# Attention in a fused layer: six heads of eight scored as three products of halves, and three copies per batch moved to another engine

## The reference

```python
q = rope(rmsnorm(x @ Wq))            # 32 query heads of 128
k, v = rope(rmsnorm(x @ Wk)), x @ Wv # 8 key heads of 128
k_all = concat(k_cache[block_table], k)   # 16 pages of 32 keys, 32 new ones: 544
v_all = concat(v_cache[block_table], v)
scores = (q . k_all) / sqrt(128), masked beyond the cache length
o = softmax(scores) @ v_all          # 4 query heads share a key head
x + o @ Wo
```

## Time and profile before

| what | value |
|---|---|
| median of 3 runs | 2431.99 us (2431.39 to 2432.4) |
| the profiled execution itself | 2430.95 us |
| its span | 2429.2 us |
| busy in the span: TensorE, VectorE, ScalarE, GpSimd | 95%, 74%, 55%, 47% |
| attention, by the timeline | 829 to 2057 us |

### The profile page before, as it was taken

One profiled execution on the slowest core, in us unless ns is written; L12 is line 12 of the kernel. 1 busy time (PEld: TensorE's weight loads), 2 busy tenths in 40 slices (PEclk: granted clock), 3 DMA queues, 4 the chain that ended last, 5 costly groups with the idle time before them and its releaser, 6 DMA issues. The chain is left out here.

```text
span 2429.2 us, 50595 instructions
## 1 busy us (share of the span) xinstructions
PE 2318.3 (95%) x14977; PEld 1934.9 (80%) x14977; DVE 1790.6 (74%) x3412; ACT 1344.7 (55%) x2635; POOL 1145.5 (47%) x1330
## 2 busy tenths in 40 slices
PE   6997899999999499999999999999999998899999
PEld 5335777777777399999999999999999997788887
DVE  4565189999999588888888888888888886522221
ACT  6563388888887355555555555555555554421111
POOL 0320044444444376777776777777777675000000
PEclk9998999999999699999999999999999999999999
DMA  9335323333332688888888888888888885843441
GB/s 313 99 102 177 103 66 108 109 109 108 108 104 79 196 280 298 289 280 290 297 289 290 277 291 288 297 294 281 285 292 296 286 292 172 256 133 96 129 138 60
DMA packets 463993, 501.42 MB, mean 206 GB/s; under 512 B 102069, under 2 KB 396981, under 8 KB 457654
## 3 DMA queue, kind: packets, MB, share of 16 engines
q1 hardware_dynamic: 427062, 366.37, 47.6%
q0 software_dynamic: 36864, 134.23, 15.8%
HBM read 404.02 MB, written 96.47 MB: 206 GB/s over the span
## 5 line engine op out<-in xcount | busy, mean ns | idle before, releaser
L1092 POOL TENSOR_TENSOR att_probs<-att_probs,att_inverse 128x512 f32<-128x512 f32 x512 | 535.1, 1045 | 289.1 <-DVE att_inverse L1288 284.5
L1196 ACT ACTIVATE att_probs<-att_probs,att_low 128x544 f32<-128x544 f32 x512 | 383.9, 750 | 515.8 <-DVE att_low L1275 454.7
L1153 PE MATMUL att_o<-att_probs_t,att_values 128*128 128x128 f32 x4096 | 540.9, 275 | 0.0
L1275 DVE CUSTOM_DVE_ANT_0 att_probs<-att_score,att_mask,att_batch_cols 128x544 f32<-128x544 f32 x512 | 399.9, 781 | 138.3 <-PE att_score L1118 99.6
L1153 PEld LDWEIGHTS att_o<-att_probs_t,att_values 128*128 128x128 f32 x4096 | 497.6, 192 | 0.0
L1284 DVE COPY att_probs_t<-att_turn 128x512 f32<-128x512 f32 x512 | 350.8, 685 | 1.2 <-PE att_turn L1133 1.2
L1078 POOL DMA_INDIRECT att_values<-L_cond_v_cache,att_v_rows_of x256 | 283.7, 1108 | 82.4 <-POOL att_v_rows_of L1074 49.7
L1118 PE MATMUL att_score<-att_keys_raw,att_queries_raw 128*128 128x288 f32 (+1 forms) x1024 | 290.7, 407 | 29.0 <-DMA att_queries_raw<-q_t 26.8
L1133 PE MATMUL att_turn<-ident,att_probs 128*128 128x128 f32 x2048 | 311.1, 274 | 1.2 <-POOL att_probs L1092 0.9
L787 PE MATMUL proj_proj<-x3t_hi,proj_w_hi 128*128 128x512 f32 x640 | 266.7, 417 | 6.9 <-DVE proj_w_lo L847 6.9
L1251 DVE TENSOR_TENSOR att_keys_lo<-att_keys_raw,att_keys_hi 128x384 fp32r<-128x384 f32 (+1 forms) x320 | 259.8, 812 | 17.6 <-ACT att_keys_hi L1189 17.6
(11 more groups left out here) (132 smaller groups left out, 4008.6 us busy)
## 6 DMA issues: line engine op xcount, KB each, us to landing
att_keys_raw<-L_cond_k_cache SPq DMA_DIRECT2D x1024, 128.0 KB
q_t<-proj_q_out SPq DMA_DIRECT2D x32, 1024.0 KB, 3.9
att_queries_raw<-q_t SPq DMA_DIRECT2D x64, 512.0 KB
o_t<-att_heads_out SPq DMA_DIRECT2D x64, 512.0 KB
out_o_raw<-o_t SPq DMA_DIRECT2D x32, 1024.0 KB, 5.8
prep_natural<-L_cond_weight SPq DMA_DIRECT2D x16, 1024.0 KB, 8.4
w_nat<-L_cond_Wq SPq DMA_DIRECT2D x8, 1024.0 KB, 5.4
v_new<-values_v_out SPq DMA_DIRECT2D x64, 128.0 KB, 2.0
```

The lines of the kernel that those rows point to most:

```text
L1092: nc.gpsimd.tensor_tensor(probs[:, k, 0:L], probs[:, k, 0:L], inverse[:, k:k + 1].to_broadcast([P, L]), ALU.mult).then_inc(probs_ready, 1)
L1153: last = nc.tensor.matmul(o, values[j][:, t, h * D:(h + 1) * D], probs_t[m % 2][:, t * P:(t + 1) * P], start=(t == 0), stop=False, skip_gr ...
L1196: nc.scalar.activation(probs[:, k, :], probs[:, k, :], ACT.Exp, bias=low[k][:, 0:1], scale=-1.0, accum_out=total[k][:, 0:1]).then_inc(exp_ ...
L1275: nc.vector.tensor_tensor_reduce(out=probs[:, k, :], in0=score_ps[:, LEFT:LEFT + KEYS], in1=mask[j][:], scale=batch_cols[j][:, h:h + 1], s ...
```

## The change

Two heads of eight stay native in place of four, so `SPLIT` is six, and each part of the keys is 3 pages of six heads (576 columns; the last part 2 pages, 384 columns), in six parts in place of five; the queries are 768 columns in place of 512. ScalarE begins with the next batch in head 1 in place of 4, VectorE in head 2 in place of 5. The copy of the turned weights goes to ScalarE for heads 1, 4 and 7 of a batch; ScalarE makes it two heads later, ahead of the exponent of that later head. VectorE keeps the other five. Since `NATIVE` is 2, the next load of keys is issued after three scored heads in place of five, and TensorE waits for the halves at head 2.

```diff
-    NATIVE = 4
-    ACT_FROM, DVE_FROM = 4, 5
+    NATIVE = 2
+    ACT_FROM, DVE_FROM = 1, 2
+    KEPT_BY_ACT = (1, 4, 7)
     SPLIT = HK - NATIVE
-    PARTS = [slice(0, 3), slice(3, 6), slice(6, 9), slice(9, 13), slice(13, NPP + 1)]
+    PARTS = [slice(0, 3), slice(3, 6), slice(6, 9), slice(9, 12), slice(12, 15), slice(15, NPP + 1)]
...
# ScalarE
+            def main_part(i, n):
+                m = n % N
+                back = i if n >= 0 else i - 1
+                act.wait_ge(turned, i * N + (n + 1))
+                act.wait_ge(weighed[m % 2], back * (N // 2) + m // 2)
+                nc.scalar.activation(probs_t[m % 2][:], turn_ps[:], ACT.Copy).then_inc(kept, 1)
...
             def pair(i, first, last_pair):
                 for n in range(N):
                     j, h = divmod(n, HK)
+                    if (n - 2) % HK in KEPT_BY_ACT and (n >= 2 or not first):
+                        main_part(i, n - 2)
                     softmax(i, n)
...
             pair(PAIRS - 1, False, True)
+            main_part(PAIRS, -1)
             new_part(PAIRS, -1)
...
# VectorE
                     mask_scores(i, n, first)
-                    if n >= 2 or not first:
+                    if (n - 2) % HK not in KEPT_BY_ACT and (n >= 2 or not first):
                         main_part(i, n - 2)
...
             main_part(PAIRS, -2)
-            main_part(PAIRS, -1)
```

## The result

The changed kernel takes **2454.23 us** in the median of four runs (2453.07 to 2456.26), against 2431.69 (2430.72 to 2432.4) before: a ratio of 1.0094, 95% interval 1.0076 to 1.0111, slower by 22.5 us. The forecast was 2464.5, its range 2421 to 2483. The profiled execution took 2456.26 us with a span of 2454.1; before it was 2430.95 with 2429.2.

The account below looks back on a forecast made before the run. TensorE looked like the bound, but GpSimd's chain sets each batch up to the turn of head 4. 62 batches at 0.5 us give 31, plus 1.5 at the start: 2464.5 us against the 2431.99 median, range 2421 to 2483.

Parts of the forecast that it names:

- TensorE's 0.24 us between T2 and T4: Saving per batch from the start of head 2's scores (T2) to head 4's (T4), inside the stretch GpSimd sets.
- I take the middle of 0.35 and 0.88: Lateness of GpSimd's product of head 4: about 0.6 us, less 0.09, so 0.5 us more per batch.
- asks first by 0.09 to 0.29: At head 5, VectorE's key subtraction asks for the port 0.09 to 0.29 us before GpSimd's product of head 4.
- I gave TensorE 0.09 us: Head 2 starts 0.09 us earlier after head 1, outside the stretch GpSimd sets; the saving left per batch.
- Later heads take nothing more: After the turn of head 4, the products of heads 5 to 7 are ready before TensorE asks.
- The start: ScalarE splits seven parts ahead of the first softmax in place of four: +1.5 us, between -0.5 and +4.
- rival 4: Keys are late at ScalarE's first split and everything behind stands; each us late costs 62; chance 0.05.
- the 1.3 us of room: Margin for the next batch's key loads: all landed after 17 us, 18.3 remain.
- The moved copies: Three copies per batch on ScalarE at about 0.586 us; 0.1 us delay in the exponent, hidden in the reciprocal's wait.
- Rivals 1 and 2: GpSimd keeps the port into the group product; second gather shorter (2422, chance 0.26) or as before (2428, chance 0.12).
- rival 1: GpSimd keeps the port into the group product, second gather may shrink towards 1.00 us; 2422, faster; chance 0.26.
- Rival 3: GpSimd keeps the port at head 3, VectorE wins at head 6; that turn waits 0.3 us; 2446; chance 0.07.

Follow-up runs that it names:

- e6: The changed kernel with GpSimd's 128x4 copy of the value rows' numbers put ahead of its product of head 2 in place of behind it: 2422.36 us.
- e2: The kernel before with only the copies of heads 1, 4 and 7 moved to ScalarE, four heads still native: 2430.21 us.
- e5: The changed kernel with six heads split but all copies left on VectorE: 2483.41 us.
- e4: On top of e2, VectorE makes the next batch's mask in head 1 in place of head 4: 2423.88 us.
- e3: The changed kernel with VectorE's reciprocal of head 4 ahead of its subtraction there: 2453.43 us.
- e1: The changed kernel without VectorE's subtraction in head 4, keys in five parts, ScalarE making the queries in head 6: 2443.92 us.
- e9: The changed kernel with five heads split, keys in four parts, no subtraction in heads 2 to 4, and the early copy of e6: 2417.87 us.
- e10: On top of e6, the next batch's gathers in heads 3, 5, 6 and 7 in place of 3, 4, 5 and 6: 2418.12 us.
- e7: The kernel before with the same early 128x4 copy as e6: 2428.49 us.

## Why the prediction was right, and where its sizes were off

**The sign and the mechanism held.** The forecast said that TensorE's 0.24 us between T2 and T4 are no gain, since the turn of head 4 hangs on GpSimd; that VectorE's subtraction of head 4 comes some hundredths of a microsecond before the group product and gets in first; and that the product of head 4 is then late. Each is in the trace: TensorE's stretch is 0.19 shorter; the reciprocal of head 2 stands 3.14 us behind T2 (1502.22), as forecast; the group product takes 0.98 in place of 0.40 (forecast 0.55 to 0.62 more); the turn of head 4 is late; e6 shortens the chain and the loss goes with it.

**The term that was mis-sized** is "I take the middle of 0.35 and 0.88". The product of head 4 starts 0.37 later than before, the lower end. Two pieces decide that. At head 4 VectorE came first (1506.40 against 1506.42), as forecast. At head 5 it did not: its subtraction is recorded from 1508.50, 0.07 before GpSimd's product of head 4 at 1508.57, and yet the product took its plain 1.05 and the subtraction 1.74. I had counted "asks first by 0.09 to 0.29" as winning. The difference from head 4 is that the subtraction started while a gather was still running (to 1508.55); at head 4 it was a product (to 1506.47). And the second gather went from 1.20 to 0.99, which the forecast had allowed for as the low end. So a batch lost 0.35 where 0.5 was forecast: 21.6 in place of 31 over 62.

**Outside that stretch** I gave TensorE 0.09 us. From the turn of head 4 to the next T2 it now takes 8.76 (1509.67 to 1518.43) or, by the mean batch, 19.40 less 10.59 = 8.81, against 19.05 less 10.22 = 8.83: of the 0.09 some 0.02 arrived in the mean. "Later heads take nothing more" was not quite right either: third and fourth gather take 1.32 in place of 1.12 each, and some 0.08 us goes around the turn of head 6 (1514.77, 0.94 behind the scores before it for 0.92; the weigh 0.49 behind it for 0.43).

**The start** was put at 1.5; 2.2 is what the batches leave over, within its bounds, and the late second set of keys (1.18 us) was in them. One later set was late as well (1.26 us at 880.06), none after it: rival 4's steady form did not happen, but the 1.3 us of room was thin, as the eight later waits of e6 show.

**The moved copies** at nothing: confirmed by e2 for four native heads. The duration was right (586 forecast, 598 measured); ScalarE was busy for 70% of the stretch where near 80% was forecast. But the forecast argued them as harmless on ScalarE only; e5 shows that they are what keeps the change from being twice as bad, which I had not said. **The subtractions** of 576 columns take 0.75 alone, as put; the queries' 768 take 0.95 to 1.07 for 1.0.

**The rivals.** Rivals 1 and 2 (GpSimd keeps the port) are excluded by the group product's mean of 699 ns; the side effect in rival 1, the shorter gather, happened all the same, and e4 shows that this alone is worth 6 to 7 us. That the sign came out right is in part luck: the forecast gave VectorE a lead of 0.08 us over the group product and it had 0.02, the same way round in all 56 batches between 900 and 2000 us. Rival 3's race at head 6 was lost by VectorE: it asks at 1510.93, GpSimd's product is at 1511.12, again behind a running gather. What I can't separate by these runs: whether the resource is the memory port itself. What they show is that each engine holds up the other, depending on who starts first, and for how long; and that it is not all of a gather that excludes, since in e6 the subtraction of head 3 (1503.27) starts 0.03 us behind the first gather, runs beside it, and both keep their 0.75 and 1.00.

## What to carry to other kernels

A saving on the engine that looks like the bound is paid out only if the stretch it lies in is that engine's own; here one wait of 0.11 us per batch marked a chain of another engine with no slack at all, and moving one 128x4 copy out of that chain (e6) turned a loss of 22 us into a gain of 8. Before work is moved between engines that exclude each other, write down the order of requests to a tenth of a microsecond: who comes first decides who waits, and taking a collision away can put it on the next instruction (e3) or open a wait on a third engine (e1). If the four-head version is kept, moving the next batch's mask (e4) is the cheapest gain, 7 us; with splits in five or six heads, e9 and e10 give 14 us over the kernel before.

## What the runs showed of the hardware that I had not expected

- **Issuing a gather is held up by VectorE too, if VectorE's instruction runs when the gather starts.** A 128x512 mask of one SBUF input that starts 0.15 us ahead of it: 1.20 us against 0.99. A 576-column subtraction that starts just ahead of it: 1.50 to 1.53. One that has its last half microsecond left: 1.31 to 1.32. In all of these the gather ends 0.85 to 0.88 us behind VectorE's instruction. Started behind the gather's start, by 0.03 us (e6, a subtraction at 1503.27) or 0.15 us (e7, the mask), they cost it nothing.
- **A subtraction that starts in the last tenths of a gather does not come first.** Started 0.05 us (1508.50, changed kernel) or 0.17 us (e1, 1505.49 against 1505.66) before the gather's end, it lets the product behind the gather run its plain 1.05 and ends 0.62 us after it. Started in the last 0.07 us of a product (1506.40 against 1506.47), 0.02 us ahead of the group product, it wins. The recorded start of an instruction is thus not the moment from which it keeps the other engine out.
- **A gather behind a wait starts late**: 0.77 us behind an instruction of its own engine, 0.97 behind TensorE (whose ends in the profile are modelled), 0.16 where the condition had long been met. With it the tiny copy took 0.96 us of the chain, from its start to the gather's.
